# First stage of a routed convolution and a scan kernel: next inputs' norms in phases 3 and 4, maps spread in two pairs

## The reference

```python
x = x + routed_conv(gn(x))        # first stage of the kernel
x = x + two_scans(gn(x))          # second stage, not touched by the change

def gn(v):                        # 32 groups of 2 channels, per image
    g = v.reshape(B, H, W, 32, 2)
    m, s = mean(g, (1, 2, 4)), var(g, (1, 2, 4))
    return ((g - m) / sqrt(s + 1e-5)).reshape(v.shape)

def routed_conv(x):               # K = 4 experts, 3 steps, 2 heads of 16
    for t in range(3):
        k, v = x @ Wk, x @ Wv     # split in heads
        attn = softmax(q . k / 4) over the 1024 pixels, per head
        logits = (sum over pixels of attn * v) @ Wmlp
        weights = softmax(masked(logits, allowed) / 1.5)
        wsel = the two largest weights, normalised; the others 0
        x_mod = x * (1 + mean_heads(attn) * 1024 * softplus(alpha))
        y = sum_e wsel[e] * (conv3x3(x_mod, We[e]) + be[e])
        allowed loses the top expert unless it is the last one
        x = y
    return x
```

## Time and profile before

| | us |
|---|---|
| median of 3 runs | 3884.75 |
| lowest, highest | 3884.1, 3887.78 |
| the profiled execution | 3886.65 |
| its span, first to last instruction | 3884.5 |

### The profile page before, as it was taken

How to read it: one execution, slowest core, us unless ns; L and a number is a source line. 1 busy time by engine, 2 the same in 40 slices (tenths; PEclk the granted TensorE clock), 3 DMA queues, 4 the chain that set the end, 5 groups by cost and what they waited for, 6 DMA issues and landing times. The chain is left out here.

```text
span 3884.5 us, 36761 instructions
## 1 busy us (share of the span) xinstructions
PE 3609.6 (93%) x9740; PEld 1388.3 (36%) x9740; DVE 3698.2 (95%) x3395; ACT 3031.5 (78%) x4614; POOL 3264.2 (84%) x1542
## 2 busy tenths in 40 slices
PE   6999998999999999999999999999999999999998
PEld 2232222333333333333333333333333333333333
DVE  6878777999999999999999999999999999999998
ACT  5677776788888888888888888888888888888885
POOL 2222223999999999999999999999999999999998
PEclk8999999999999999999999999999999999999999
DMA  4242335999889899989999989989999998999986
GB/s 115 55 123 55 111 112 177 363 349 346 344 345 355 345 348 347 350 348 346 347 354 351 351 349 348 347 347 345 356 351 350 348 349 346 345 348 354 353 339 251
DMA packets 203137, 1181.22 MB, mean 304 GB/s; under 512 B 30929, under 2 KB 31729, under 8 KB 68785
## 3 DMA queue, kind: packets, MB, share of 16 engines
q1 hardware_dynamic: 200128, 1177.64, 80.3%
q10 hardware_dynamic: 2800, 1.23, 0.1%
HBM read 1144.03 MB, written 34.73 MB: 303 GB/s over the span
## 5 line engine op out<-in xcount | busy, mean ns | idle before, releaser
L1565 POOL TENSOR_TENSOR read<-state,bc_all 128x1024 f32<-128x1024 f32 x1024 | 2395.8, 2363 | 108.1 <-DVE state L1629 105.2
L1629 DVE TENSOR_TENSOR_SCAN state<-decays,p_drive 128x1024 f32<-128x1024 f32 x1024 | 2289.0, 2273 | 18.6 <-ACT p_drive L1464 4.8
L1334 PE MATMUL p_y<-read,ident 128*128 128x512 f32 x4096 | 1955.7, 604 | 16.0 <-POOL read L1565 8.8
L1456 ACT ACTIVATE decays<-dt,wa 128x496 f32<-128x496 f32 x2048 | 1336.9, 702 | 75.2 <-DVE state L1629 72.7
L1334 PEld LDWEIGHTS p_y<-read,ident 128*128 128x128 f32 x4096 | 739.5, 190 | 1053.4 <-issue 774.2
L1616 DVE TENSOR_TENSOR p_drive<-bc_all,p_dtx 128x1024 f32<-128x1024 f32 x768 | 908.6, 1213 | 0.0
L1582 POOL TENSOR_TENSOR pool_drive<-dtx,bc_all 128x1024 f32<-128x1024 f32 x256 | 603.7, 2358 | 3.7 <-DMA bc_all<-bc_scratch 3.7
L1464 ACT COPY p_drive<-pool_drive 128x1024 f32<-128x1024 f32 x256 | 260.8, 1019 | 415.0 <-DVE state L1629 415.0
L785 POOL TENSOR_TENSOR pad<-map_all,xc 128x512 f32<-128x512 f32 x96 | 130.5, 1391 | 484.1 <-DMA map_all<-map_scratch 484.1
L566 PE MATMUL p_conv<-pad,wm 128*64 128x512 f32 x1152 | 268.7, 601 | 23.9 <-issue 23.8
L1330 PE MATMUL p_y<-xconv,d_diag 128*128 128x512 f32 x256 | 143.9, 644 | 156.6 <-DVE gated L1639 156.6
(11 more groups left out here) (163 smaller groups left out, 3067.9 us busy)
## 6 DMA issues: line engine op xcount, KB each, us to landing
bc_all<-bc_scratch SPq DMA_DIRECT2D x1024, 1024.0 KB, 6.9
map_all<-map_scratch SPq DMA_DIRECT2D x48, 512.0 KB, 5.8
norm_rows<-xn SPq DMA_DIRECT2D x32, 280.0 KB, 6.1
norm_in<-norm_rows SPq DMA_DIRECT2D x64, 140.0 KB, 7.8
norm_in<-norm_rows SPq DMA_DIRECT2D x64, 139.8 KB, 7.9
fresh<-in_x SPq DMA_DIRECT2D x32, 256.0 KB, 6.7
x<-in_x SPq DMA_DIRECT2D x32, 256.0 KB, 3.4
mid_x<-x SPq DMA_DIRECT2D x32, 256.0 KB, 6.6
```

The lines of the kernel that those rows point to most:

```text
L1334: nc.tensor.matmul(p_y[:], ident[:], read[:, s % DEEP, :], start=False, stop=(s == N - 1)).then_inc(y_added, 1)
L1456: nc.scalar.activation(decays[:, s % DEEP, :].rearrange("p (q t) -> p q t", t=SIDE)[:, :, 1:], dt[b][:, :, 1:], ACT.Exp, scale=wa[m][:, s: ...
L1565: nc.gpsimd.tensor_tensor(read[:, s % DEEP:s % DEEP + 2, :], state[:, s % DEEP:s % DEEP + 2, :], bc_all[s // CHUNK][:, :, 1, :], ALU.mult) ...
L1629: nc.vector.tensor_tensor_scan(state[:, at:at + 2, :].rearrange("p s n -> p (s n)"), decays[:, at:at + 2, :].rearrange("p s n -> p (s n)") ...
```

## The change

It edits the first stage in these places:
- The norm of the next body's inputs is computed in phases 3 (team 0) and 4 (team 1) and applied where it was, in phases 5 and 0. Its scale and shift get their own columns of `gn` (10 to 13). `norm_in_phase` becomes `norm_made` and `norm_applied`. The "out" norms and the very first two "in" norms stay.
- `map_all` is filled by four DMAs of two images and one half each, instead of two DMAs of four images, and each pair has its own semaphore. GpSimd waits for the first pair before image 0 and for the second before image 2.
- ScalarE makes `map_rows` before `prob` and step_out 1, instead of after them.
- VectorE makes `mod_w` before the `mix_last` of image 2 of the phase before, instead of between those of images 2 and 3.

```diff
-    gn = sb("gn", [128, 10, TEAM])
+    gn = sb("gn", [128, 14, TEAM])
-    map_loaded = sem("s1_map_loaded")
+    map_loaded = [sem(f"s1_map_loaded{n}") for n in two]
...
-    def norm_in_phase(i, k, before, after):
+    def norm_made(i, k, before):
+        if k in (3, 4) and i < BODIES - 1:
+            return (4 * i + k - 1, "in", k - 3)
+        if k == 0 and not before:
+            return (1, "in", 1)
+        if k in (1, 2) and before:
+            return (4 * i - 1 + k, "out", k - 1)
+        return None
+
+    def norm_applied(i, k, before, after):
...
+    def norm_place(kind, pair):
+        return (10 + 2 * pair, 11 + 2 * pair) if kind == "in" else (9, 7)
...
         ge(sp, padded_ready, 4 * P)
         sp.wait_ge(map_stored, 16 * P + 16)
-            for h in two:
-                rows = map_scratch[TEAM * h:TEAM * h + TEAM].rearrange("a n -> (a n)")
-                sp.dma_start(map_all[CH * h:CH * h + CH, :, :].rearrange("p a n -> p (a n)"),
-                             rows.partition_broadcast(CH)).then_inc(map_loaded, 16)
+            for n in two:
+                for h in two:
+                    at = TEAM * h + 2 * n
+                    rows = map_scratch[at:at + 2].rearrange("a n -> (a n)")
+                    sp.dma_start(map_all[CH * h:CH * h + CH, 2 * n:2 * n + 2, :].rearrange("p a n -> p (a n)"),
+                                 rows.partition_broadcast(CH)).then_inc(map_loaded[n], 16)
...
@@ scalar_program, slot @@
-            if norm:
-                group_root(act, norm[0])
+            if made:
+                group_root(act, made[0])
+            act.wait_ge(modul_done, P + 1)
+            ge(act, map_stored, 16 * P)
+            nc.scalar.activation(map_rows[:], p_modul[0:2 * TEAM, :], ACT.Identity, bias=1.0).then_inc(map_ready, 1)
             act.wait_ge(wexp_in, P + 1)
             nc.scalar.activation(prob[:], logit[:], ACT.Exp, scale=1.0 / 1.5).then_inc(wexp_done, 1)
             if steps:
                 step_out(i, k - 1, 1)
-            act.wait_ge(modul_done, P + 1)
-            ge(act, map_stored, 16 * P)
-            nc.scalar.activation(map_rows[:], p_modul[0:2 * TEAM, :], ACT.Identity, bias=1.0).then_inc(map_ready, 1)
...
-            if norm:
-                norm_apply(act, *norm)
+            if applied:
+                norm_apply(act, *applied)
...
@@ gpsimd_program, slot @@
-            pool.wait_ge(map_loaded, 32 * P + 32)
             for a in team:
+                if a % 2 == 0:
+                    pool.wait_ge(map_loaded[a // 2], 32 * P + 32)
...
@@ vector_program, slot @@
-            norm = norm_in_phase(i, k, before, after)
+            norm = norm_made(i, k, before)
...
-                body = i + 1 if k == PHASES - 1 else i
+                body = i + 1 if k in (3, 4) else i
...
-                free = {5: (x_out, 2 * i), 0: (x_norm, 2 * i + 1), 1: (x_norm, 2 * i + 2), 2: (x_out, 2 * i - 1)}[k]
+                free = {0: None, 1: (x_out, 2 * i - 2), 2: (x_out, 2 * i - 1), 3: (x_norm, 2 * i + 1), 4: (x_norm, 2 * i + 2)}[k]
...
             if norm:
                 norm_variance(dve, number)
-            late(mix_last, 2)
             chain(dve, nc.vector.tensor_scalar(kmap[:], r[:], float(PIX), c["gain"][0:R, 3:4], ALU.mult, ALU.mult))
             ge(dve, modul_done, P)
             nc.vector.tensor_scalar(mod_w[:], c["spread"][:], kmap[:], None, ALU.mult).then_inc(mod_w_ready, 1)
+            late(mix_last, 2)
             late(mix_last, 3)
...
             if norm:
-                norm_scale(dve, number)
+                norm_scale(dve, number, kind, pair)
```

More of the change, by code:

```diff
@@ L685, in norm_apply @@
         act.wait_ge(gn_scale, n + 1)
+        scale, shifted_by = norm_place(kind, pair)
         for a in team:
@@ L688, in norm_apply @@
                         (x1[pair][a][:].rearrange("p (j w) -> p j w", w=SIDE), xn[pair][a][:, :, PAD:]))
-            o = nc.scalar.activation(dst, src, ACT.Identity, scale=gn[:, 9, a:a + 1], bias=gn[:, 7, a:a + 1])
+            o = nc.scalar.activation(dst, src, ACT.Identity, scale=gn[:, scale, a:a + 1], bias=gn[:, shifted_by, a:a + 1])
         o.then_inc(x_norm if kind == "in" else x_out, 1)
@@ L727, in slot @@
             P, g = i * PHASES + k, k % 2
-            norm = norm_in_phase(i, k, before, after)
+            made, applied = norm_made(i, k, before), norm_applied(i, k, before, after)
             steps = 1 <= k <= PHASES - 2
@@ L822, in norm_variance, with norm_scale @@
         nc.vector.tensor_scalar(gn[:, 3, :], p_gn[:, P_VAR], 1e-5, None, ALU.add).then_inc(gn_v, 1)
-    def norm_scale(dve, n):
+    def norm_scale(dve, n, kind="out", pair=0):
+        scale, shifted_by = norm_place(kind, pair)
         dve.wait_ge(gn_rs, n + 1)
-        for src_r, dst_r in ((5, 8), (8, 9)):
+        for src_r, dst_r in ((5, 8), (8, scale)):
             chain(dve, nc.vector.tensor_tensor(gn[:, 6, :], gn[:, src_r, :], gn[:, src_r, :], ALU.mult))
@@ L831, in norm_scale @@
             chain(dve, nc.vector.tensor_tensor(gn[:, dst_r, :], gn[:, 6, :], gn[:, src_r, :], ALU.mult))
-        nc.vector.scalar_tensor_tensor(gn[:, 7, :], gn[:, 0, :], -1.0, gn[:, 9, :],
+        nc.vector.scalar_tensor_tensor(gn[:, shifted_by, :], gn[:, 0, :], -1.0, gn[:, scale, :],
                                        ALU.mult, ALU.mult).then_inc(gn_scale, 1)
@@ L871, in norm_first @@
         norm_variance(dve, 0)
-        norm_scale(dve, 0)
+        norm_scale(dve, 0, "in", 0)
         for a in team:
```

## The result

The changed kernel took 3937.51 us (median of 4 runs, 3935.96 to 3940.12) against 3884.48: a ratio of 1.0134, 95% interval 1.0121 to 1.0147, 53 us slower. I had forecast slower, but 3923 with an upper end of 3935, 2.5 us too low. The profiled execution took 3935.96, its span is 3933.8, which is 49.3 above the span before.

What follows compares the result with a forecast made beforehand. First-stage phases were taken as bound by the loop of map rows, DMA, pad and TensorE, with VectorE's mixing loop close behind. Terms 39.6 - 1.1 - 3.0 + 1.8 + 1 = +38.3 on 3886.65, less 1.9, gave 3923 us; range 3873 to 3935.

Steps and rivals of the forecast that it cites:

- 12 norm phases: Phases that make a norm, mostly k = 1 to 4: period 28.0 against a mean of 24.7, +3.3 each, +39.6.
- 4 plain phases: k = 1, 2 of the first body, 3, 4 of the last: two mixing operations slowed, -0.27 each, -1.1.
- 3 phases k = 5: Mixing starts earlier without norm_scale, three mixing operations left for pads: period 25.7 against 26.65, -1.0 each.
- 3 phases k = 0: All four pads come in from the third mixing operation on, statistics of k = 1 behind: +0.6 each, +1.8.
- Four pads get between them: Norm phases: pads take turns between the last four mixing operations, which end at 23.83 instead of 19.67; chance 0.45.
- rival A: First pair not there by 16.47, so only two or three turns in norm phases: 3911 or 3898 us; chance 0.25.
- Rival C: Pairs do not separate, first lands as late as the whole did, pads start at 18.3 to 18.7: 3871 us; chance 0.10.
- Rival B: VectorE keeps the turn at mixing boundaries, pads wait for the mixing's end: 3867 us; chance 0.10.
- First phase 0: The first phase of the first stage was to neither win nor lose time: 0 in the sum.
- The granted clock is 1.00 in all of them: Read from the five profiled phases of the kernel before: clock 1.00 in each.
- the last phase, +1 in my sum: Last phase: first mixing would meet three pads instead of none, mixing behind it would be free; estimated +1.
- +0.52 on the mixing loop: Norm phases: prob waits for map rows and comes at 9.70 instead of 9.18, delaying the mixing by 0.52.

Runs made afterwards that it cites:

- e1: Changed kernel with GpSimd's first pad of each phase also waiting for mix_last of image 1: 3883.89 us, ratio 0.9992 to the kernel before.
- e2: Changed kernel with GpSimd waiting for both pairs of the maps before its first pad: 3876.30 us, ratio 0.9975 to the kernel before.
- e4: Kernel before with only the maps spread in two pairs (four DMAs, two semaphores): 3895.02 us, ratio 1.0028.
- e5: Kernel before with only the reorder, map rows ahead of prob and mod_w ahead of mix_last 2: 3887.94 us, ratio 1.0002.
- e6: Changed kernel without the reorder of map rows, prob and mod_w: 3887.18 us, ratio 0.9998 to the kernel before.
- e7: Changed kernel with four filler matmuls in TensorE's wait for mixed weights after each norm phase: 3931.05 us, ratio 1.0112 to the kernel before.
- e3: Kernel before with only the next inputs' norms moved to phases 3 and 4: 3874.84 us, ratio 0.9970.
- e8: Changed kernel without the reorder, norm_scale of moved norms behind the mixing, first pad held to mix_last of image 0: 3872.87 us, ratio 0.9961 to the kernel before.
- e9: Changed kernel without the reorder, first pad held to mix_last of image 0, norm_scale ahead of the mixing: 3864.42 us, ratio 0.9944 to the kernel before.
- O: The order part of the change, map rows and mod_w earlier; alone on the kernel before 3887.94 us, ratio 1.0002.
- P: The pairs part of the change, maps spread by four DMAs in two pairs; alone on the kernel before 3895.02 us, ratio 1.0028.

## Why the prediction was wrong, and where it was right

By the profiles, with phases taken from exp to exp, the 49.3 us divide so:

| term | predicted | measured |
|---|---|---|
| 12 norm phases | +39.6 | +40.0 |
| 4 plain phases | -1.1 | +2.4 |
| 3 phases k = 5 | -3.0 | -1.7 |
| 3 phases k = 0 | +1.8 | +1.1 |
| first phase | 0 | +3.7 |
| before the first exp | 0 | +0.3 |
| from the last phase's exp to the end | +1 | +3.5 |
| sum | +38.3 | +49.3 |

**The mechanism was right.** "Four pads get between them" held in nine of the twelve norm phases, and their period was 27.9 to 28.0 for the forecast 28.0, but for the one of 29.63. Three had three turns (mix_last ending at 20.5 after exp instead of 21.5) and 26.9: there the first pad came after the boundary that I had it reach by 0.27, which is rival A. That +39.6 met +40.0 is in part luck. The twelve phases took 24.5 before on the mean and not 24.7, which would have made it +42; the three short ones took 3.1 off, and the clock put 1.7 on. e1 and e2 took all or most of the pads out of the mixing and with them 54 and 61 us, and e4 and e5 came out within 0.5 us of what the same arithmetic gave for each kind of phase, apart from single phases with a lower clock or a turn more or less. Rival C fell with a first pad 16.53 after the start of the count and not at 18. Rival B fell in the changed kernel, where no pad waited for the end of the mixing.

**But B is what the first phase does.** In eight of the twelve kernels, the kernel before among them, the first pad of all met mixing, and each time VectorE kept its pace and the pad waited. The longest such pad is that of e6, GpSimd's timeline first and VectorE's below it:

```profile
39.11 8.45 POOL L800 TENSOR_TENSOR pad<-map_all,xc 128x512 f32<-128x512 f32 x3 [29.81 <-DMA map_all<-map_scratch]
39.12 1.67 DVE L866 SCALAR_TENSOR_TENSOR mix<-we_sb,wsel,mix 128x640 f32<-128x640 f32 x2
40.71 1.67 DVE L871 SCALAR_TENSOR_TENSOR mix<-we_sb,wsel,mix 128x640 f32<-128x640 f32 x2
42.30 1.66 DVE L878 SCALAR_TENSOR_TENSOR wm<-we_sb,wsel,mix 128x640 f32<-128x640 f32 x2
```

The first pad alone takes 5.99 of the 8.45, and six mixing operations pass beside it at 0.80 intervals. That it is the first use of the instruction is a guess that no run tests. In the changed kernel the first pad met no mixing and took 1.26, and from the second pad on the turns were strict.

**The step that failed first: "First phase 0".** It lasted 32.2, not 28.6. The windows of the kernel before and of the changed kernel:

```profile
24.04:52.60 28.56, 18.91 (x56) 6.40 (x58) 19.14 (x74) 13.23 (x24) 7.20 (x4) 0.64 0.28 75
24.32:56.56 32.24, 20.06 (x56) 6.48 (x58) 22.12 (x74) 13.13 (x24) 5.53 (x4) 0.58 0.26 75
```

Its modulation weights have no mix_last ahead of them, so map rows came at 7.91 after exp as before (7.90) and prob moved from 6.84 to 8.52, as in e5. Mixing then began 2.6 later (0.9 of it a small instruction that waited out a pad) and, with two turns, ended 4.7 later, at 24.08. conv_main of image 0 so started 2.7 later, and its 12 matmuls took 5.39 instead of 4.29, since the granted clock, already low in this phase, was lower still. I had taken one phase kind for all.

**The second: "The granted clock is 1.00 in all of them", carried over in silence.** It is so for those five windows, but the sum used it for phases with longer waits, and for the first phase, where it was 0.64 before. Each turn lengthens TensorE's wait for mixed weights. Behind most of these waits the granted clock was at half, 1.2 GHz, for part of the next few us (0.72 and 0.62 in the two windows above), and matmuls there took up to twice as long. Where TensorE was not on the path this was hidden. It was paid in the 29.63 phase (1.7), in the last plain phase (26.9: one turn more than forecast, +1.0, and 1.7 more from conv_anti to the next exp), in the first phase (1.1) and, with 0.3 each, in k = 5 of the second and third body. That makes about 5 of the 11 us by which the sum missed. e7, which keeps TensorE busy, has a span 5.6 us shorter, though its turns also fell otherwise. The fourth plain phase is also where "two operations left" was short: the first pad came a mixing operation earlier and three turns fell in. In k = 5 four turns fell in the second and third body where I had three, which is the rest of that line; in k = 0 there were four once and three twice where I had four.

**The third, in part open: the last phase, +1 in my sum.** From its exp to the end of the span the changed kernel took 3.5 more. From that exp to the first scan of the second stage it took 51.4 where the kernel before took 49.5: 1.9 more, and e1, e3, e8 and e9, whose pads meet the mixing least, took 0.1 to 0.4 more. The other 1.7 comes behind the first scan. There e3, whose last phase is the old one, also took 2.5 more and the others up to 2.9, so that it is not the turns; what it is was not tried. Last, 3.7 of the 53 us are in the medians and not in the two profiles: the first profile stands 2.2 above its median and the second 1.6 below its own.

**The reorder** was costed nearly right as +0.52 on the mixing loop (mixing begins 0.6 later in the norm phases) and -1.1 for the maps (0.85 in norm phases, 1.2 in plain ones), but I did not see that the same 1.1 us, small in the sum, decides the number of turns: without O norm phases have two turns (25.3), with it three or four (27 to 28). O and P each shift pads toward the mixing, and the cost goes by steps of one turn, by where they arrive.

The Trainium skill ("SBUF — State Buffer", Who interferes with whom) says that a VectorE instruction with two SBUF inputs contends with a GpSimd instruction that reads SBUF; the 1.9 against 0.87 above agrees, everywhere but at the first pad. So do step_last, which reads PSUM, one image in SBUF and a bias, and takes 0.74 beside pads and 0.75 without, and the statistics, 2.47 for four beside pads as without. It also has tensor_scalar contend when it runs in a two-port mode: L848 in e8, at 1.21, agrees, if it ran in that mode. The fixed 2.0 us for a DMA in the Trainium skill ("DMA: Bandwidth & Descriptors", Anatomy of one DMA), which that section gives for DMAs issued by GpSimd while these are issued by SP, would have put the first pad 1.3 sooner than I did; it came 5.2 us after the first issue, 0.2 later than mine.

## What to carry to other kernels

Before data is made to arrive sooner, look at what its consumer runs beside from then on: if it is a GpSimd operation and VectorE works with two SBUF inputs, each encounter cost VectorE 1.04 to 1.09 us here, beside a GpSimd operation of 1.24, even for an instruction of four elements. Hold the early consumer until the last such instruction has started (e9, 21 us below e6), and look in which phases an early start pays by itself (the plain phases of e4, 22.95 for 24.4). And cost each kind of phase, the first and last among them, with the clock that TensorE will have after the new waits.

## What the runs showed of the hardware

From the second pad of a kernel on, turns are strict and depend on arrival: a pad that waits gets in at the next boundary between VectorE's instructions, VectorE at the one after, so that an operation of 0.80 comes at 1.84 intervals, four in a row in the timeline of k = 3 of the changed kernel. The first pad of the kernel is the exception: it waited up to 5.99 us beside mixing that kept its pace, in all eight kernels where the two met. An instruction of four elements a partition pays the same as one of 640 (1.20 to 1.25 against 0.16).

TensorE waited 2.08 to 2.83 us for mixed weights 13 times in the changed kernel. Behind ten of these waits the next 12 matmuls took 4.3 to 4.5 us (5.4 in the first phase) instead of 2.80, with the granted clock at half for a part of them. Behind three, of 2.42, 2.75 and 2.42, they took 2.80, and in one of these phases later matmuls were slow. The wait of 1.56 in the kernel before left them at 2.80, a wait of 1.95 in e1 did so in k = 3 and not in k = 4. So no length of a wait alone decides it in these runs.
